# Macaron layer on Trainium2: the feed-forward halves unrolled, routed two batches at a time, expert weights applied by GpSimd

## The chip, the cores and the metric

The kernel runs on one core of a Trainium2 chip. The metric is the device time of the whole program in microseconds (us), from its first to its last instruction with what lies around them. Lower is better.

## What is computed

The input x has 8 batches of 512 tokens of 128 features, in float32. Three residual blocks follow each other: half a mixture-of-experts feed-forward, attention with 16 heads of 64, and the same feed-forward again. Only the feed-forward is touched by the change:

```python
x = x + 0.5 * ffn(layernorm(x)); x = x + attn(layernorm(x)); x = x + 0.5 * ffn(layernorm(x))
# ffn, over all N = 4096 tokens
scores = softmax(x @ gate_w.T); topk_w, topk_idx = top_k(scores, 2); topk_w /= topk_w.sum()
pos = cumsum(one_hot(topk_idx)) - 1; keep = pos < capacity       # capacity 1280 for each of 8 experts
comb = scatter(topk_w * keep)                                     # (N, 8)
y  = sum_e comb[:, e] * (silu(x @ we_gate[e].T) * (x @ we_up[e].T)) @ we_down[e].T
sh = silu(x @ ws_gate.T) * (x @ ws_up.T) @ ws_down.T              # shared, 256 wide = 2 groups
```

The running count in pos goes through all tokens in order, so batches have to be routed one after another.

## The kernel before

The work lies features by tokens: a batch is a 128x512 tile, one PSUM bank. The feed-forward has 10 groups per batch, 2 shared and 8 experts, each 128 wide. Every product that must hold float32 accuracy is made of three fp32r terms: both operands are split into a high part (a ScalarE copy to fp32r) and a low part (a subtraction), and high x high, low x high and high x low are added in one bank.

A group takes nine 512-column matmuls and this chain: gate product (L375), SiLU on ScalarE (L496), product with the up half on VectorE (`gated`, L635), for an expert the product with its weight row (`weighted`, L643), high part on ScalarE (L505), low part on GpSimd (L728), down product (L418). The weight row of an expert is spread over 128 partitions by a matmul of its own with a selection matrix (`weights`, L410). The down product of a group runs four groups behind its gate product (`LAG_Y`), the high part two groups behind.

Between the groups lie, for each batch: layer norm of a later batch on VectorE (L259, small steps L230 to L250, L265), transposes (L347), gate logits as three matmuls with 8 rows (L355), a ScalarE copy (L486) and transposes back (L362), some 20 small routing steps on VectorE (L562 to L616), among them four over all 8x8 pairs of experts (L576 to L582) that rank the scores, the positions by small matmuls (L382 to L387), transposes of three bf16 parts of the weights (L396), a copy (L622), the output's copy (L511), its transposes (L427) and the residual (L650).

Each engine runs a list written out by hand; semaphores connect them. `groups` runs the groups through a loop with a register for the batch; tables such as `ROUTE_AT` say at which group which small step stands. Attention is written out without loops and hands over when all of x is done (L650, last batch); the second feed-forward begins after attention's last residual (L1084).

Of the kernel before, what the change touches and what calls it, by code (L numbers as in the profile page):

```python
# [32 lines left out]
NH = 5  # L33
SETS = 3
SPLIT3 = 3
RSQRT_MAGIC = 0x5F3759DF
NEWTON = 3
ROUTE_STEPS = 21
LN_STAGES = 7 + 3 * NEWTON
LN_STEPS = TT + 7 + 2 + 4 * NEWTON + TT - 1  # L40
# [21 lines left out]
def macaron(nc, x, w_gate_up, w_down, gate_t, w_qk, w_v, w_out, b_out, fproj, bproj,  # L62
            rope, fourier, consts, consts_b, sel, rows, out):
    with ExitStack() as ctx:
# [3 lines left out]
        def sem(name):  # L68
# [9 lines left out]
        gate_hi = sb("gate_hi", [P, E], F32R)  # L78
        gate_lo = sb("gate_lo", [P, E], F32R)
# [9 lines left out]
        ident_b = sb("ident_b", [P, P], BF16)  # L89
        before_b = sb("before_b", [P, P], BF16)  # L90
        ones_b = sb("ones_b", [P, P], BF16)
        lower = sb("lower", [P, E, E])
        sel_b = sb("sel_b", [P, E, P], BF16)
# [5 lines left out]
                   sb(f"rs_{n}", [P, n]), sb(f"rsi_{n}", [P, n], I32), sb(f"nt_{n}", [P, 3, n])) for n in (TT, LATER)}  # L99
        stats, mean, rs = own[TT][0], own[TT][2], own[TT][4]  # L100
        stats_all, mean_all, rs_all = own[LATER][0], own[LATER][2], own[LATER][4]
# [6 lines left out]
        st_v = work[:, 4096:4096 + INNER]  # L108
        st_gu = work[:, 4096 + INNER:4096 + INNER + 2 * GROUPS * P]

        o_t = sb("o_t", [P, 2, T])
        comb_t = sb("comb_t", [P, T], BF16)
        route = sb("route", [P, 8, TT, E])
        rec_all = sb("rec_all", [P, 2, T])
        pairs = rec_all[:, 0].rearrange("p (n m) -> p n m", n=2)
        pair_gt, pair_ge = (pairs[:, n].rearrange("p (t a e) -> p t a e", t=TT, a=E) for n in range(2))
        small = sb("small", [P, 8, TT])
        mask_b = sb("mask_b", [P, TT, E], BF16)
# [3 lines left out]
        comb3 = sb("comb3", [P, TT, SPLIT3, E], BF16)  # L122
# [3 lines left out]
        hid_hi, hid_lo = qk_h[:, SETS - 1], qk_l[:, SETS - 1]  # L126
# [3 lines left out]
        act_g, prod = o_t[:, 0:2, :], turn[:, 1]  # L130
# [11 lines left out]
        st_down = work[:, 4096 + INNER + 2 * GROUPS * P:4096 + INNER + 3 * GROUPS * P]  # L142
        free = 4096 + INNER + 3 * GROUPS * P
        fourier_s, fproj_s = work[0:NF, free:free + T], work[0:NF, free + T:free + T + P]
# [6 lines left out]
        in_first, in_fourier, in_x0 = sem("in_first"), sem("in_fourier"), sem("in_x0")  # L151
# [9 lines left out]
        def setup_sync(sp):  # L161

            sp.dma_start(x_tok[:, 0], x[0].rearrange("(t p) d -> p t d", p=P)).then_inc(in_x0, 16)
            sp.dma_start(ident[:], consts[0]).then_inc(in_first, 16)
            sp.dma_start(gate_w[:], gate_t).then_inc(in_first, 16)
            sp.dma_start(st_gu, w_gate_up).then_inc(in_ffn, 16)
            sp.dma_start(fourier_s, fourier).then_inc(in_fourier, 16)
            sp.dma_start(fproj_s, fproj).then_inc(in_fourier, 16)
            sp.dma_start(bproj_s[:], bproj).then_inc(in_fourier, 16)
            sp.dma_start(lower[:].rearrange("p a b -> p (a b)"), consts[1][:, 0:E * E]).then_inc(in_small, 16)  # L170
            sp.dma_start(st_down, w_down).then_inc(in_ffn, 16)
            sp.dma_start(before_b[:], consts_b[0]).then_inc(in_small, 16)
            sp.dma_start(ident_b[:], consts_b[1]).then_inc(in_small, 16)
            sp.dma_start(sel_b[:].rearrange("p e m -> p (e m)"), sel).then_inc(in_small, 16)
            for b in range(1, B):
                sp.dma_start(x_tok[:, b], x[b].rearrange("(t p) d -> p t d", p=P)).then_inc(in_x, 16)
# [7 lines left out]
        def setup_act(act):  # L184
            act.wait_ge(in_first, 32)
            nc.scalar.activation(gate_hi[:], gate_w[:], ACT.Copy).then_inc(w_hi_ready, 1)

            act.wait_ge(in_fourier, 48)
            act.wait_ge(fenc_ps, 1)
            nc.scalar.activation(fenc[:], bank[6][:], ACT.Identity, bias=bproj_s[:, 0:1]).then_inc(fenc_ready, 1)  # L190
# [84 lines left out]


        def ffn(tag, last, follow=None):

# [1070 lines left out]
```

## Time and profile before

| | us |
|---|---|
| median of 3 runs (1409.71 to 1411.80) | 1411.39 |
| the profiled execution, its own time | 1412.86 |
| its span, first to last instruction | 1410.8 |
| first feed-forward, to its last residual | 260.8 |
| attention, from there to its last residual | 896.8 |
| second feed-forward, from there to its last residual | 249.7 |

The last three lines are differences of the starts of residual rows on VectorE (260.82, 1157.60, 1407.26). A profile page gives, for each engine, busy time, share of the span and instructions; a timeline row gives start, duration, engine, line, operation, output and inputs, and in brackets the idle time before it with what ended it. PE is TensorE, DVE is VectorE, ACT is ScalarE, POOL is GpSimd.

### The profile page before, as it was taken

Reading aid. Unit: us, or ns where it says so; the run is one execution under the profiler, and the core shown is the slowest. Engines: PE = TensorE matmul, PEld = TensorE weight load, DVE = VectorE, ACT = ScalarE, POOL = GpSimd, SP = SyncE. Lnnn points to the kernel's source line nnn. Section 1 sums busy time; section 2 is a strip of 40 time slices with the busy share of each in tenths; the row PEclk is TensorE's granted clock in tenths of the full one; section 3 lists DMA queues with packets and bytes.
Section 4 is the critical chain, followed back from the end, with each engine's and each line's share of the span. In section 5 each row is a group of like instructions: output and inputs, shape, how many; then the busy total and the mean of one; then the engine's idle time right before and its main releaser. Section 6 shows DMA issues by size and latency. Waiting matters only on the chain.

```text
span 1410.8 us, 25300 instructions
## 1 busy us (share of the span) xinstructions
PE 1297.9 (92%) x8258; PEld 828.9 (59%) x8258; DVE 1000.4 (71%) x1900; ACT 703.9 (50%) x1042; POOL 926.1 (66%) x684
## 2 busy tenths in 40 slices
PE   4999889689999999999999999999999937988997
PEld 2666666346656656666566566566566525666665
DVE  7889988687666666666666666666666426998896
ACT  3565555245455555555555545545545404555553
POOL 0444444577888888888888788788888512444444
PEclk9999999899999999999999999999999967999999
DMA  6000000123233232232232332332332210000000
GB/s 206 1 0 0 0 0 0 30 46 69 48 68 68 48 69 65 51 69 61 55 69 57 59 69 51 65 69 47 69 69 47 39 24 0 8 7 15 7 7 16
DMA packets 101418, 61.71 MB, mean 44 GB/s; under 512 B 75280, under 2 KB 84016, under 8 KB 101072
## 3 DMA queue, kind: packets, MB, share of 16 engines
q1 hardware_dynamic: 101328, 60.52, 19.8%
q8 instruction: 56, 0.92, 0.3%
q14 instruction: 34, 0.28, 0.1%
HBM read 24.30 MB, written 2.62 MB: 19 GB/s over the span
## 4 chain that ended last, share of the span: by engine, by line
PE 68%; DVE 8%; issue 3%; DMA 1%; DVEq 0%; POOL 0%; ACT 0%; SPq 0%; POOLq 0%; ACTq 0%
PE banks L919 16%; PE banks L902 13%; PE banks L934 6%; PE banks L878 6%; PE banks L843 6%; PE banks L907 4%; PE banks L375 4%; PE banks L943 4%; PE banks L862 3%; PE banks L418 2%; PE banks L885 1%; PE banks L410 1%; DVE xn L265 1%; DVE neg_max L1064 1%; DVE work L643 1%
## 5 line engine op out<-in xcount | busy, mean ns | idle before, releaser
L728 POOL TENSOR_TENSOR qk_l<-work,qk_h 128x512 fp32r<-128x512 f32 x160 | 206.3, 1293 | 301.2 <-ACT qk_h L505 299.8
L1064 DVE TENSOR_REDUCE neg_max<-banks 128x2 f32<-128x1024 f32 x256 | 313.4, 1224 | 102.5 <-PE banks L878 96.3
L1000 ACT ACTIVATE work<-banks 128x1024 f32<-128x1024 f32 x256 | 250.1, 1025 | 168.3 <-PE banks L907 168.3
L1148 POOL TENSOR_TENSOR turn<-turn,side_turned 128x512 f32<-128x512 f32 x128 | 160.7, 1276 | 129.1 <-DMA side_turned<-side 129.1
L919 PE MATMUL banks<-work 128*64 128x512 f32 x1024 | 233.8, 598 | 0.0
L1142 POOL TENSOR_TENSOR turn<-turn,fenc 128x512 f32<-128x512 f32 x128 | 162.4, 1291 | 12.6 <-DVE side L1057 8.9
L1153 POOL TENSOR_TENSOR qk_l<-turn,qk_h 128x512 fp32r<-128x512 f32 x128 | 162.1, 1289 | 0.9 <-ACT qk_h L1005 0.9
L1158 POOL TENSOR_TENSOR work<-work 128x1024 f32<-128x1024 f32 x64 | 153.1, 2392 | 6.2 <-PE banks L919 6.2
L919 PEld LDWEIGHTS banks<-work 128*64 128x64 f32 x1024 | 67.8, 136 | 132.8 <-issue 110.0
L505 ACT ACTIVATE qk_h<-work 128x512 fp32r<-128x512 f32 x160 | 100.6, 629 | 71.5 <-DVE work L643 62.1
L375 PE MATMUL banks<-x_hi,gu_hi 128*128 (+1 forms) x320 | 133.5, 417 | 2.6 <-DVE work L635 2.2
L375 PE MATMUL banks<-x_hi,gu_lo 128*128 (+1 forms) x320 | 128.9, 403 | 0.0
L375 PE MATMUL banks<-x_lo,gu_hi 128*128 (+1 forms) x320 | 127.6, 399 | 0.0
L878 PE MATMUL banks<-qk_h 64*128 64x512 f32 x512 | 116.7, 452 | 11.3 <-DVE neg_max L1064 8.3
L496 ACT ACTIVATE o_t<-banks 128x512 f32<-128x512 f32 x160 | 94.7, 592 | 63.8 <-PE banks L375 54.0
L1070 DVE TENSOR_TENSOR shift<-banks,own_rows 128x512 fp32r<-128x512 f32 x64 | 44.2, 691 | 111.0 <-PE banks L885 111.0
L643 DVE TENSOR_TENSOR work<-turn,banks 128x512 f32<-128x512 f32 x128 | 87.4, 684 | 35.2 <-PE banks L410 29.1
L1005 ACT ACTIVATE qk_h<-turn 128x512 fp32r<-128x512 f32 x128 | 80.5, 629 | 53.6 <-POOL turn L1148 53.5
L902 PE MATMUL banks<-qk_h 64*128 64x512 f32 x512 | 101.9, 395 | 1.4 <-DVE side L1057 1.4
L1057 DVE TENSOR_TENSOR turn<-banks,rope_t 128x1024 f32<-128x1024 f32 x63 | 77.1, 1224 | 36.6 <-PE banks L843 35.5
L902 PE MATMUL banks<-qk_h,qk_l 64*128 64x512 f32 x512 | 101.3, 392 | 0.0
L902 PE MATMUL banks<-qk_l,qk_h 64*128 64x512 f32 x512 | 101.3, 392 | 0.0
(149 smaller groups left out, 2517.6 us busy)
## 6 DMA issues: line engine op xcount, KB each, us to landing
side_turned<-side SPq DMA_DIRECT2D x256, 128.0 KB, 3.1
rec_all<-rec_d SPq DMA_DIRECT2D x128, 128.0 KB, 3.0
x_tok<-in_x SPq DMA_DIRECT2D x8, 256.0 KB, 5.8
out<-x_tok SPq DMA_DIRECT2D x8, 256.0 KB, 2.3
work<-in_w_gate_up SPq DMA_DIRECT2D x1, 1280.0 KB, 6.6
work<-in_w_qk SPq DMA_DIRECT2D x1, 1024.0 KB, 7.1
den_d<-den_rows SPq DMA_DIRECT2D x64, 4.0 KB
den_c<-den_d SPq DMA_DIRECT2D x64, 4.0 KB, 1.9
```

The costliest lines, as they stand in the source:

```text
L375: ins = nc.tensor.matmul(dst[:], w[:, j + k, :], of_batch(a, b), start=(n == 0), stop=(n == 2))
L643: nc.vector.tensor_tensor(hid[:, k % NH, :], prod[:, k % 2, :], C[k % 2][:], ALU.mult).then_inc(s["hidden"], 1)
L728: nc.gpsimd.tensor_tensor(hid_lo[:, k % 2, :], hid[:, k % NH, :], hid_hi[:, k % 2, :], ALU.subtract).then_inc(s["hid_lo_ready"], 1)
L878: ins = nc.tensor.matmul(M2[:, h, :], qk_h[OWN[h], g % SETS, Q, qt * P:(qt + 1) * P], qk_h[OWN[h], g % SETS, K, :], start=True, stop=True)
L902: nc.tensor.matmul(S[kt][:, h, :], k[OWN[h], g % SETS, K, keys], q[OWN[h], g % SETS, Q, :], start=(i == 0), stop=False)
L919: ins = nc.tensor.matmul(O[OWN[h], :], v_all[:, kt, n * DH:(n + 1) * DH], pt[:, g % 2, kt, h * T:(h + 1) * T], start=(kt == 0), stop=(kt = ...
L1000: nc.scalar.activation(pt[:, g % 2, kt, :], S[kt].rearrange("p h q -> p (h q)"), ACT.Exp, scale=QSCALE).then_inc(s["probs"], 1)
L1064: nc.vector.tensor_reduce(neg_max[:, g % 2, qt::DH], M2, AX.X, ALU.max, negate=True).then_inc(s["maxes"], 1)
L1142: nc.gpsimd.tensor_tensor(turn[:, g % 2, part], turn[:, g % 2, part], fenc[:], ALU.add).then_inc(s["with_fourier"], 1)
L1148: nc.gpsimd.tensor_tensor(turn[:, g % 2, part], turn[:, g % 2, part], side_turned[:, part], ALU.add).then_inc(done, 1)
L1153: return nc.gpsimd.tensor_tensor(qk_l[:, g % SETS, part], turn[:, g % 2, part], qk_h[:, g % SETS, part], ALU.subtract)
L1158: nc.gpsimd.tensor_tensor(pt[:, g % 2, 0, :], pt[:, g % 2, 0, :], pt[:, g % 2, 1, :], ALU.add).then_inc(s["first_sum"], 1)
```

## The change

Only `ffn`, the setup and the first steps of attention that overlap the first feed-forward are rewritten.

- The loop over batches is gone: `UNITS` lists all 80 (batch, group) pairs, and each engine runs `period(i)` for i in that list. Of the first two batches the four shared groups come first, then the experts of each.
- Layer norm, softmax, ranking and positions are done for two batches (8 token tiles) at once, at fixed places in a window of 20 periods. The top two are found by maximum, comparison with the maximum and a code that breaks ties, in place of the 8x8 pairs. There are 24 routing stages per window (before 20 per batch).
- The logits come from 16 matmuls per window with the tokens stationary and 16 moving columns; the three matmuls, the copy and the transposes back are gone.
- The weight rows go through DRAM: one transpose (L398) and one ScalarE copy, one DMA out, then for each batch two DMAs of 1 MB that spread the rows over all partitions (`share_in`). The eight selection matmuls, the bf16 split, its transposes and L622 are gone.
- An expert's SiLU output is multiplied by its weight row on GpSimd (`weighted`, L709), and VectorE multiplies that by the up half (`gated`, L643). The low part of the product is subtracted on VectorE (`hidden_low`, L647) instead of GpSimd.
- The normalised tokens are written by ScalarE (`tokens`, L485, four per batch).
- The down product of a group stands two groups behind its gate product (`LAG` 2), the high part one.

```diff
-                    for k in range(OPEN, GROUPS):
-                        step(b, k, True, True)
...
+NORM_AT = {0: range(0, 4), 1: range(4, 10), 2: range(10, 16)}
+ROUTE_AT = {8: range(0, 4), 9: range(4, 9), 10: range(9, 14), 11: range(14, 19), 12: range(19, 22), 13: range(22, 24)}
+FIRST_ROUTE_AT = {0: range(4, 14), 1: range(14, 22), 2: range(22, 24)}
...
                 def period(i):
+                    if i < N:
+                        gate_up(i)
...
+                    if c < CHUNKS and q == LOGITS_AT:
+                        logits(c)
+                    if c < CHUNKS and q == POSITIONS_AT:
+                        positions(c)
+                    if c < CHUNKS and q == SHARES_AT:
+                        turn_shares(c)
+                    if i == FIRST_POSITIONS_AT:
+                        positions(0)
+                    if i == FIRST_SHARES_AT:
+                        turn_shares(0)
+                    if 0 <= i - LAG < N:
+                        down(i - LAG)
...
+                def gated(i):
...
+                    source = act_g[:, i % 2, :] if g < NSH else act_w[experts(i) % 2]
+                    tt(hid[i % NH], source, U[i % 2][:], ALU.mult).then_inc(s["gated"], 1)
+
+                def hidden_low(i):
+                    dve.wait_ge(s["hid_hi_ready"], i + 1)
+                    tt(hid_lo[:, i % 2, :], hid[i % NH], hid_hi[:, i % 2, :], ALU.subtract)\
+                        .then_inc(s["hid_lo_ready"], 1)
...
+                    if i < N:
+                        gated(i)
+                    c, q = chunk(i)
+                    if 0 <= i - 1 < N:
+                        hidden_low(i - 1)
...
-                    nc.gpsimd.tensor_tensor(hid_lo[:, k % 2, :], hid[:, k % NH, :], hid_hi[:, k % 2, :],
-                                            ALU.subtract).then_inc(s["hid_lo_ready"], 1)
...
+                    nc.gpsimd.tensor_tensor(tiled(act_w[experts(i) % 2]), tiled(act_g[:, i % 2, :]),
+                                            share[b % 2][:, (g - NSH) // HALF_E, :, (g - NSH) % HALF_E, :],
+                                            ALU.mult).then_inc(s["weighted"], 1)
```

VectorE's order for two expert groups in mid-stream, before (turn is the unweighted product, work the weighted one):

```order
L635 TENSOR_TENSOR turn<-o_t,banks 128x512
L639 REGISTER_ALU
L642 REGISTER_ALU
L643 TENSOR_TENSOR work<-turn,banks 128x512
```

and in the change (rec_all and den_rows hold GpSimd's weighted SiLU, qk_l the low part):

```order
L643 TENSOR_TENSOR o_raw<-rec_all,banks 128x512
L647 TENSOR_TENSOR qk_l<-turn,qk_h 128x512
L643 TENSOR_TENSOR o_raw<-den_rows,banks 128x512
L647 TENSOR_TENSOR qk_l<-o_raw,qk_h 128x512
```

Both large VectorE steps of a group read PSUM before; now the second reads two SBUF tiles.

VectorE's order at the opening, between the first group's product and the mask of the first batch, before:

```order
L635 TENSOR_TENSOR work<-o_t,banks 128x512
L215 TENSOR_TENSOR down_lo<-work,down_hi 128x1280
L584 TENSOR_REDUCE route<-rec_all 128x32
L259 BN_STATS stats<-x_tok 128x6 x4
L586 TENSOR_SCALAR mask_b<-route 128x32
```

and the start of the same piece in the change, in which 34 rows lie between the first product and the mask (L611):

```order
L643 TENSOR_TENSOR turn<-o_t,banks 128x512
L248 TENSOR_TENSOR down_lo<-work,down_hi 128x1280
L566 BN_STATS stats<-x_tok 128x6 x8
L263 TENSOR_TENSOR mv<-stats 128x8
L264 TENSOR_TENSOR mv<-stats 128x8
L265 TENSOR_TENSOR ve<-stats 128x8
L267 TENSOR_SCALAR mean<-mv 128x8
L268 TENSOR_SCALAR rs<-ve 128x8
L269 TENSOR_TENSOR nt<-mv 128x8
L271 SCALAR_TENSOR_TENSOR ve<-nt,rs 128x8
L591 TENSOR_REDUCE small<-side_turned 128x8
```

The norm of the next two batches now stands ahead of the first mask.

TensorE's order there (the shapes are output partitions by columns):

```order
L408 MATMUL banks<-qk_l,gu_hi 128x512
L384 MATMUL banks<-count_b,ones_b 128x64
L387 MATMUL banks<-mask_b,ones_b 128x56
L387 MATMUL banks<-mask_b,ones_b 128x48
L387 MATMUL banks<-mask_b,ones_b 128x40
L387 MATMUL banks<-mask_b,ones_b 128x32
L387 MATMUL banks<-mask_b,ones_b 128x24
L387 MATMUL banks<-mask_b,ones_b 128x16
L387 MATMUL banks<-mask_b,ones_b 128x8
L390 MATMUL banks<-mask_b,before_b 128x64
L408 MATMUL banks<-qk_h,gu_hi 128x512
```

The positions, which wait for the mask, now stand behind the second group's gate and up products and ahead of the third's; before, they stood behind two and a half groups.

## Rows read from the trace of the kernel before

**Rows 1.** Busy time, share and instructions of each engine (page).

```profile
PE 1297.9 (92%) x8258; PEld 828.9 (59%) x8258; DVE 1000.4 (71%) x1900; ACT 703.9 (50%) x1042; POOL 926.1 (66%) x684
```

**Rows 2.** One batch in mid-stream, busy time of each engine (windows).

```profile
108.19:136.89 28.70, 26.05 (x124) 18.71 (x122) 25.88 (x76) 15.95 (x28) 12.91 (x11) 1.00 0.00 0
```

**Rows 3.** Where batches 0, 2 and 6 begin and each feed-forward ends (timeline).

```profile
18.74 0.77 PE L375 MATMUL banks<-x_hi,gu_hi 128*128 128x512 f32 x1 [0.25 <-issue]
...
79.53 0.40 PE L375 MATMUL banks<-x_hi,gu_hi 128*128 x1
...
79.77 0.40 PE L375 MATMUL banks<-x_hi,gu_lo 128*128 x1
...
194.27 0.40 PE L375 MATMUL banks<-x_hi,gu_hi 128*128 x1
...
260.82 0.69 DVE L650 TENSOR_TENSOR x_tok<-banks,x_tok 128x512 f32<-128x512 f32 x1 [5.04 <-PE banks L427]
...
1169.55 0.78 PE L375 MATMUL banks<-x_hi,gu_hi 128*128 128x512 f32 x1
...
1229.59 0.40 PE L375 MATMUL banks<-x_hi,gu_hi 128*128 x1
...
1344.32 0.40 PE L375 MATMUL banks<-x_hi,gu_hi 128*128 x1
...
1407.26 0.69 DVE L650 TENSOR_TENSOR x_tok<-banks,x_tok 128x512 f32<-128x512 f32 x1 [5.04 <-PE banks L427]
```

**Rows 4.** TensorE in one batch, its waits and its transposes (timeline).

```profile
114.59 0.19 PE L382 MATMUL banks<-mask_b,before_b 128*128 128x32 bf16 x1 [0.88 <-DVE mask_b L586]
...
119.21 0.39 PE L396 MATMUL banks<-ident_b,comb 128*24 128x128 bf16 x4 [0.73 <-DVE comb L616]
...
122.01 0.39 PE L410 MATMUL banks<-comb_t,sel_b 128*128 128x512 bf16 x1 [1.03 <-DVE comb_t L622]
...
123.68 0.60 PE L347 MATMUL banks<-ident,xn 128*128 128x128 f32 x4
...
124.04 0.48 PE L375 MATMUL banks<-x_hi,gu_hi 128*128 x1
```

**Rows 5.** VectorE beside GpSimd, and the same line alone (timeline).

```profile
108.75 1.28 POOL L728 TENSOR_TENSOR qk_l<-work,qk_h 128x512 fp32r<-128x512 f32 x1 [0.17 <-ACT qk_h L505]
...
108.78 1.53 DVE L577 TENSOR_TENSOR rec_all<-route 128x256 f32<-128x256 f32 x1
...
20.41 0.42 DVE L577 TENSOR_TENSOR rec_all<-route 128x256 f32<-128x256 f32 x1
```

**Rows 6.** One group's chain at the end of the second feed-forward (timeline).

```profile
1395.90 0.39 PE L375 MATMUL banks<-x_lo,gu_hi 128*128 128x512 f32 x1
...
1396.33 0.60 ACT L496 ACTIVATE o_t<-banks 128x512 f32<-128x512 f32 x1 [0.41 <-PE banks L375]
...
1400.95 1.28 DVE L643 TENSOR_TENSOR work<-turn,banks 128x512 f32<-128x512 f32 x2
...
1402.37 1.27 POOL L728 TENSOR_TENSOR qk_l<-work,qk_h 128x512 fp32r<-128x512 f32 x1 [0.74 <-ACT qk_h L505]
```

**Rows 7.** Norm and transposes at the start of the second feed-forward (timeline).

```profile
1158.53 0.87 DVE L259 BATCH_NORM_STATS2 stats<-x_tok 128x6 f32<-128x128 f32 x4
...
1160.32 0.17 DVE L241 TENSOR_SCALAR rsi<-ve 128x4 int32<-128x4 int32 x1
...
1160.52 0.17 DVE L243 TENSOR_SCALAR rs<-rsi 128x4 int32<-128x4 int32 x1
...
1164.00 1.08 PE L347 MATMUL banks<-ident,xn 128*128 128x128 f32 x4 [6.50 <-DVE xn L265]
```

**Rows 8.** A split on VectorE, tokens on ScalarE (timeline), a large DMA (page).

```profile
22.35 1.48 DVE L215 TENSOR_TENSOR down_lo<-work,down_hi 128x1280 fp32r<-128x1280 f32 x1
...
336.75 1.64 ACT L1012 ACTIVATE xn<-x_tok,shift_all,rs 128x128 f32<-128x128 f32 x4
...
work<-in_w_gate_up SPq DMA_DIRECT2D x1, 1280.0 KB, 6.6
```

More of the change, by code:

```diff
@@ new lines, in chunk, with experts, nth_expert, last_of @@
+            def chunk(i):
+                return i // WINDOW + 1, i % WINDOW
+            def experts(i):
+                return sum(1 for b, g in UNITS[0:i] if g >= NSH)
+            def nth_expert(n):
+                return [i for i in range(N) if UNITS[i][1] >= NSH][n] if n >= 0 else -1
+            def last_of(b):
+                return max(i for i in range(N) if UNITS[i][0] == b)
+            def first_of(b):
+                return min(i for i in range(N) if UNITS[i][0] == b)
+            def turned_at(i):
+                return next((b for b in range(B) if last_of(b) + LAG + 1 == i), None)
@@ L466, in pe @@
                 after_attention(pe)
                 pe.wait_ge(in_first, 32)
[L468 removed]
+                for b in range(CB):
+                    front(b)
                 pe.wait_ge(w_lo_ready, 1)
[L470 to L472 removed]
                 pe.wait_ge(consts_ready, 5)
[L474 to L478 removed]
+                logits(0)
@@ new lines, in pe, with fronts_before, turns_before @@
+                pe.wait_ge(in_small, 16 * 2)
+                if not last:
+                    fourier_terms(pe)
+                    pe.wait_ge(w_lo_ready, 2)
+                    pe.wait_ge(fenc_ready, 1)
+                for i in range(N + LAG + 2):
+                    period(i)
+            def fronts_before(b):
+                at = last_of(b) + LAG + 1
+                return CB + sum(1 for i in range(at) if batch_at(i, FRONT_AT) is not None)
+            def turns_before(b):
+                at = next((i for i in range(N) if batch_at(i, FRONT_AT) == b), -1)
+                return sum(1 for i in range(at + 1) if turned_at(i) is not None)
@@ L531, in end @@
[L531 to L548 removed]
+                    nc.scalar.activation(xh(b), XT[:], ACT.Copy).then_inc(s["x_hi_ready"], 1)
@@ L742, in sync @@
-            def sync(sp):
+                if not last:
+                    dve.wait_ge(in_x0, 16 * CB)
+                for n in range(LN_STAGES):
+                    norm(n, 0)
+                if not last:
+                    gate_low(dve)
+                for b in range(CB):
+                    x_low(b)
+                if not last:
+                    gate_up_low(dve, 0)
+                    dve.wait_ge(in_x, 16 * (B - CB))
+                dve.wait_ge(in_small, 16 * 2)
+                for n in range(4):
+                    route(n, 0)
```

819 lines of the change are left out of this document (389 added, 430 removed).

## The prediction

> **What bounds the kernel now.** The page comes first: TensorE is busy 92% of the span, VectorE 71% [rows 1]. That mixes attention, which the change leaves alone, with the two feed-forwards, so the table of windows comes next: one batch takes 28.70 us, in which TensorE shows 26.05 us and VectorE 25.88 [rows 2]. Both are nearly full. The timeline tells what ends last. TensorE's matmuls start 0.23 us apart (79.53 to 79.77, [rows 3]); a group has nine of them, 2.10 us, and with the weight matmul of an expert 2.33. In each batch TensorE stands still three times, 0.88, 0.73 and 1.03 us, each time for a routing result of VectorE: the mask, the bf16 weights, their copy [rows 4]. So the groups are bound by TensorE and the gaps by VectorE's routing. From batch 2 to batch 6, four batches take 194.27 - 79.53 = 114.7 us, two of them 57.4 (second half: 1344.32 - 1229.59, the same) [rows 3].
>
> A third thing is seen in VectorE's rows: L577 takes 0.42 us alone and 1.53 us where GpSimd started 0.03 us ahead of it; it ends 0.28 us after GpSimd does [rows 5]. VectorE steps that read two SBUF tiles wait for a running GpSimd step. The large steps (L635, L643) read PSUM and are not held. The Trainium skill ("SBUF — State Buffer", Who interferes with whom) states this as a lock: a VectorE instruction with two SBUF inputs and a GpSimd instruction that reads SBUF exclude each other, in both directions. These rows agree for one direction; the other is not seen here.
>
> **What is taken off TensorE.** Per batch: eight weight matmuls, 8 x 0.23 = 1.9 us; twelve small transposes become four fewer for logits and four fewer for weights, at 0.09 each (four in 124.04 - 123.68 = 0.36 [rows 4]), 0.7 us; three logit matmuls (0.7) against sixteen small ones per two batches. Those have no row of their kind; the bounds are nearly nothing (16 of 512 columns) and 0.23 (a full one). I take 0.09, the transposes' pitch, since both load a 128-wide stationary tile each time: 1.4 us per two batches. TensorE's work falls from about 25.5 to 22.9 us per batch, which for 16 batches would be 41 us. The question is what VectorE, ScalarE and GpSimd let it have.
>
> **An expert's group in the change.** VectorE now does `gated` and `hidden_low`, the latter with two SBUF inputs, and GpSimd's `weighted` for the next group lies between them. Two large VectorE steps take 1.28 us where one takes 0.69, so they start 0.60 apart; a GpSimd step of this size takes 1.28 [rows 5, 6]. If the two exclude each other, the loop is 0.60 (gated) + 0.60 (hidden_low) + 1.28 (weighted) + 0.04 (hand-off) = 2.52 us. The chain gives nearly the same: the SiLU starts 0.43 us after the third gate matmul starts [rows 6], that is 0.90 after the group's start; SiLU 0.60, hand-off 0.08, GpSimd 1.28, 0.04, gated 0.60, hidden_low of the group before 0.69, 0.05: its down product starts 4.24 us into the group after it and takes 0.70. Two periods in 4.94 are 2.47. So an expert costs 2.52 where it cost 2.33; a shared group stays 2.10. Window of 20: 16 x 2.52 + 4 x 2.10 = 48.7 us.
>
> **What else a window holds.** Small dependent VectorE steps start 0.20 us apart (1160.32 to 1160.52 [rows 7]); with 64 elements 0.26.
> - Mask (period 12): TensorE comes to `positions` 1.4 us into its period, VectorE is at five routing stages (1.3) behind the group before, done 5.5 us after that group's start: 4.4 us for the period, +1.9.
> - Weights (period 14): the step before them reads two SBUF tiles and waits for GpSimd: +1.5.
> - Logits, 1.4 us against 0.4 of slack: +1.0.
> - Tokens on ScalarE, 1.64 us for four [rows 8], twice, ahead of the next SiLU: 2 x 1.2.
> - Statistics of eight tiles (0.87 for four [rows 7]) in a shared period: +0.4.
>
> Sum 7.2: a window takes 55.9 against 57.4, and the two middle windows of each feed-forward give 2.8 us. The residual, the low part of x and the statistics cost nothing more since they lie in the 1.28 us in which VectorE waits for GpSimd; without that cover they would cost 0.6 each.
>
> **The opening.** First gate product: four more statistics (0.87), a second set of tokens (1.64), its transposes at the lower clock (1.08 for four against 0.60 [rows 4]) and its copy come before the logits, which save a copy and transposes: +3.0 in each half. Then TensorE runs two groups (2.8 us) and meets `positions`. VectorE reaches the mask after: first product at 3.0 (before, the down split follows it at 22.35 [rows 8], so it starts at 21.75, 3.0 after 18.74 [rows 3]), 0.6, the down split 1.4 (1.48 [rows 8]), statistics 1.6, three norm stages 0.8, ten routing stages 2.5, a product and a subtraction 1.2, the second half of the gate split 1.4, six norm stages 1.3, five routing stages 1.3: 15.1. The wait is 11.5 us allowing for the slower clock, 8.7 in the second half, which has no splits. The third group then waits for the weights behind six norm stages: +4.9. The weights go out to DRAM and 1 MB comes back (1.28 MB took 6.6 us [rows 8]), about 9 us with both hand-offs, of which three groups hide some 5: +4. First window: 48.7 + 7.2 + 11.5 + 4.9 + 4 = 76.3 against 79.53 - 18.74 = 60.8, +15.5; second half 73.5 against 1229.59 - 1169.55 = 60.0, +13.5 [rows 3].
>
> **The end.** No routing follows the last two batches, and they have no window extras: 48.7 plus 5.5 for the last chain. Against 1407.26 - 1344.32 = 62.9 that is -8.7; in the first half attention's first norm and projections lie there too, about 6.5 us: 60.7 against 260.82 - 194.27 = 66.6, -5.9 [rows 3].
>
> **Sum.** First half 3.0 + 15.5 - 2.8 - 5.9 = +9.8; second 3.0 + 13.5 - 2.8 - 8.7 = +5.0; attention 0. Together +14.8 on the profiled execution's 1412.9; the median of the runs lies 1.5 below it, so 1411.4 + 14.8 = **1426 us**.
>
> By the skill's rule in both directions the sum stays. Were there no exclusion at all, it would be the second rival below.
>
> **Rivals.**
> 1. *Every routing step with two SBUF inputs waits for a GpSimd step* and all of that reaches TensorE. One such wait adds 1.1 us to L577 [rows 5], and thirteen of the 24 stages are of that kind. If three or four more in each of the six windows that have routing reach the chain, that is 4 us each: 1426 + 24 = 1450. For: [rows 5]. Against: during a window's shared groups GpSimd is idle, and I have charged the two that TensorE waits for.
> 2. *Faster:* GpSimd's product and VectorE's subtraction run beside each other, or start in an order in which neither waits, so the routing stages slip in. The place is the middle window: at 2.47 us per expert with the extras halved it takes 47.9 + 3.6 = 51.5, 4.4 less; six windows, openings included, give 26.4 and the two ends 0.8 each, 28 in all: 1398. It decides at 2.5 us less per window than I have (14.8 / 6). For: TensorE has 2.6 us less work per batch. Against: [rows 5], and the chain alone holds 2.47.
> 3. *Balance:* windows near 53.4 us pay for the openings, 1411. That is how it would look if the small logit matmuls cost next to nothing and most of the tokens' time were hidden.
>
> **How the numbers follow.** Forecast (1414 to 1442) 0.58; rival 1 0.17; rival 2 0.18; rival 3 0.07. Within 0.2% (2.8 us, about what a measurement of this kernel can tell from no change) is 0.07, faster 0.18, slower 0.75. Unknown prices: logits at nothing or 0.23 per matmul, -11 or +18 us over eight rounds, less what waits cover, so -6 to +10; the return of the weights, 3 to 12 us each half. The range 1396 to 1452 takes in both rivals' values and leaves a fifth out.
>
> **What would show it.** Gate products of experts 2.5 us apart; `hidden_low` (L647) longer than 0.69 us or `weighted` late behind it; one TensorE wait of 9 to 12 us before L384 at each opening and one near 3 before L398; in mid-stream waits before L384 and L398 near 2; two batches near 56 us; the last two batches 6 to 9 us shorter than before. It would be wrong if experts ran 2.1 to 2.3 apart, if the opening wait were under 5 us, or if the logits L377 and L378 took over 3 us per window.

## The result, and the profile of the changed kernel

| | before | change | |
|---|---|---|---|
| median of 4 runs each (us) | 1410.55 | 1457.34 | ratio 1.0334, interval 1.0316 to 1.0352 |
| span of the profiled execution | 1410.8 | 1454.5 | +43.7 |
| first feed-forward, to its last residual | 260.8 | 283.6 | +22.8 |
| attention | 896.8 | 901.3 | +4.5 |
| second feed-forward | 249.7 | 266.2 | +16.5 |

The forecast was 1426 with a range of 1396 to 1452: the direction was right, the size was not. The page's first lines (busy time of each engine, and TensorE's granted clock in 40 slices) answer to [rows 1]:

```profile
PE 1298.6 (89%) x8082; PEld 843.5 (58%) x8082; DVE 914.3 (63%) x1504; ACT 698.6 (48%) x1076; POOL 890.5 (61%) x652
...
PEclk9799999969999999999999999999999956999999
...
work<-share SPq DMA_DIRECT2D x32, 1024.0 KB, 9.1
```

VectorE's busy time fell by 86 us, and the kernel became slower: less work on an engine gains nothing where the order of steps holds the time. The timeline rows that answer to [rows 3], the first gate products of each window of 20 groups (a "period" below is the time from one group's first gate product to the next's) and the residuals that end attention and both halves:

```profile
23.82 0.77 PE L408 MATMUL banks<-qk_h,gu_hi 128*128 128x512 f32 x1 [0.89 <-issue]
...
102.85 0.39 PE L408 MATMUL banks<-x_hi,gu_hi 128*128 128x512 f32 x1
...
221.02 0.40 PE L408 MATMUL banks<-x_hi,gu_hi 128*128 128x512 f32 x1
...
1202.18 0.77 PE L408 MATMUL banks<-qk_h,gu_hi 128*128 128x512 f32 x1
...
1278.89 0.39 PE L408 MATMUL banks<-x_hi,gu_hi 128*128 128x512 f32 x1
...
1337.68 0.40 PE L408 MATMUL banks<-qk_h,gu_hi 128*128 128x512 f32 x1
...
1396.43 0.39 PE L408 MATMUL banks<-x_hi,gu_hi 128*128 128x512 f32 x1
```

```profile
283.58 0.69 DVE L653 TENSOR_TENSOR x_tok<-banks,x_tok 128x512 f32<-128x512 f32 x1 [2.40 <-PE banks L428]
...
1184.88 0.69 DVE L1104 TENSOR_TENSOR x_tok<-banks,x_tok 128x512 f32<-128x512 f32 x1 [8.80 <-PE banks L963]
...
1451.05 0.69 DVE L653 TENSOR_TENSOR x_tok<-banks,x_tok 128x512 f32<-128x512 f32 x1 [2.40 <-PE banks L428]
```

From their differences, each against the same stretch of before:

| stretch | first half | forecast | second half | forecast |
|---|---|---|---|---|
| start | +5.1 | +3.0 | +5.3 | +3.0 |
| opening window | 79.0: +18.2 | +15.5 | 76.7: +16.7 | +13.5 |
| two middle windows | 118.2: +3.4 | -2.8 | 117.5: +2.8 | -2.8 |
| end | 62.6: -4.0 | -5.9 | 54.6: -8.3 | -8.7 |

With attention's +4.5 that makes the span's 43.7. The opening is where the time is; the middle is where the forecast had the wrong sign.

**The opening.** TensorE's first waits (timeline):

```profile
38.88 0.23 PE L384 MATMUL banks<-count_b,ones_b 128*128 128x64 bf16 x1 [10.51 <-DVE mask_b L611]
...
44.95 0.42 PE L398 MATMUL banks<-ident,comb_w 128*64 128x128 f32 x1 [2.84 <-DVE comb_w L625]
```

VectorE had its first product at 26.82 and the mask at 38.60, 11.8 us later, with the norm of the next batches in between. GpSimd's first product started at 54.52, 9.6 us behind the transpose of the weights at 44.95 (forecast: about 9). The 9.1 us of the page's line is the median of 32 transfers of 1 MB, of which up to four are issued together.

**Mid-stream.** Most experts are 2.47 to 2.6 us apart, as forecast. VectorE and GpSimd there (timeline):

```profile
1333.05 0.69 DVE L643 TENSOR_TENSOR turn<-den_rows,banks 128x512 f32<-128x512 f32 x1 [1.27 <-POOL den_rows L709]
1333.65 0.68 DVE L647 TENSOR_TENSOR qk_l<-turn,qk_h 128x512 fp32r<-128x512 f32 x1
1335.53 0.69 DVE L643 TENSOR_TENSOR o_raw<-rec_all,banks 128x512 f32<-128x512 f32 x1 [1.19 <-POOL rec_all L709]
```

```profile
1331.73 1.29 POOL L709 TENSOR_TENSOR den_rows<-o_t,work 128x512 f32<-128x512 f32 x1 [1.27 <-ACT o_t L508]
1334.21 1.29 POOL L709 TENSOR_TENSOR rec_all<-o_t,work 128x512 f32<-128x512 f32 x1 [1.19 <-ACT o_t L508]
```

VectorE stands still for 1.2 us in each group, waiting for the product, then does the product and the low part in one go; the low part of the group before had been free to start earlier but stands behind. These rows fit both explanations of the forecast, the chain (2.47) and the exclusion (2.52).

### The profile page after: what moved, and what is told of

It reads as the page before. It is cut to its first block and busy times, and to the rows that moved or that the text cites. A ratio compares the mean times of both kernels' runs of the same rounds, so it can differ in the third digit from the quotient of the medians.

```text
span 1454.5 us, 22616 instructions
## 1 busy us (share of the span) xinstructions
PE 1298.6 (89%) x8082; PEld 843.5 (58%) x8082; DVE 914.3 (63%) x1504; ACT 698.6 (48%) x1076; POOL 890.5 (61%) x652
## 5 line engine op out<-in xcount | busy, mean ns | idle before, releaser
L709 POOL TENSOR_TENSOR rec_all<-o_t,work 128x512 f32<-128x512 f32 x64 | 86.8, 1356 | 266.5 <-DMA work<-share 102.5
L1162 POOL TENSOR_TENSOR turn<-turn,fenc 128x512 f32<-128x512 f32 x128 | 162.1, 1291 | 16.5 <-DVE side L1077 11.1
L709 POOL TENSOR_TENSOR den_rows<-o_t,work 128x512 f32<-128x512 f32 x64 | 84.7, 1323 | 104.7 <-ACT o_t L508 104.7
L419 PE MATMUL banks<-qk_h,down_hi 128*128 128x512 f32 x160 | 78.2, 489 | 45.8 <-DVE qk_l L647 43.1
L927 PE MATMUL banks<-shift,ones_r 64*128 64x512 f32 x512 | 102.6, 393 | 0.0
L1185 POOL TENSOR_TENSOR o_t<-o_raw,rec_all 128x512 f32<-128x512 f32 x64 | 81.7, 1276 | 27.2 <-DMA rec_all<-rec_d 27.2
L954 PE MATMUL banks<-work,ones_f 128*32 128x256 f32 x1536 | 96.2, 383 | 0.1
```

What stands on the lines that cost most here:

```text
L709: nc.gpsimd.tensor_tensor(tiled(act_w[experts(i) % 2]), tiled(act_g[:, i % 2, :]), share[b % 2][:, (g - NSH) // HALF_E, :, (g - NSH) % HAL ...
L927: ins = nc.tensor.matmul(S[kt][:, h, :], ones_r[OWN[h], :], shift[OWN[h], g % 2, :], start=False, stop=True)
L954: ins = nc.tensor.matmul(W[c:c + 32, 0:HALF], ones_f[:], pt[:, g % 2, kt, first:first + HALF], start=(n == 0), stop=(n == 2))
L1162: nc.gpsimd.tensor_tensor(turn[:, g % 2, part], turn[:, g % 2, part], fenc[:], ALU.add).then_inc(s["with_fourier"], 1)
```

## The experiments

All are timed against the kernel before in the same session; ratios to be compared are those to before. Its median lay between 1410.55 and 1412.87 us in these sessions, so differences in us between two experiments carry some 2 us of that.

**1. The norm behind the first mask.**

```diff
-FIRST_ROUTE_AT = {0: range(4, 14), 1: range(14, 22), 2: range(22, 24)}
+FIRST_ROUTE_AT = {0: range(4, 19), 1: range(19, 24)}
+FIRST_NORM_AT = {1: range(0, 10), 2: range(10, 16)}
...
-                        for n in NORM_AT.get(q, ()):
+                        for n in (FIRST_NORM_AT if c == 1 else NORM_AT).get(q, ()):
```

> Change as it is, but in the opening of each half the norm of the next two batches stands behind the first mask and not ahead of it. Theory A (the opening's two long stalls are VectorE work that lies ahead of the mask): eight statistics and ten small norm stages, about 5 us, leave the path to the first positions; the second period falls from 12.7 and 10.4 us to about 8 and 6, the third stays near 7, and the whole time falls by 8 to 10 us, to 1448 (ratio to before near 1.027). Rival B (the norm only shifts the stall, since the tokens, the logits and the shares of the next batches come later by as much): the openings stay at 79 and 77 us and the time within 2 us of 1457.

1445.58 us, ratio 1.0226 (1.0208 to 1.0243). TensorE's waits in the first opening (timeline):

```profile
32.77 0.23 PE L385 MATMUL banks<-count_b,ones_b 128*128 128x64 bf16 x1 [3.41 <-DVE mask_b L612]
...
40.51 0.42 PE L399 MATMUL banks<-ident,comb_w 128*64 128x128 f32 x1 [4.50 <-DVE comb_w L626]
```

The wait for the mask fell from 10.51 to 3.41, the next one grew by 1.7; the opening windows measured 73.6 and 72.0, 5.4 and 4.7 less. The second period fell further than expected (to 6.5 and 5.5 us), but the third did not stay near 7: it grew from 7.3 and 6.6 to 8.9 and 7.6. Theory A holds: this much of the opening was order alone.

**2. The low part before the product.**

```diff
-                    if i < N:
-                        gated(i)
                     c, q = chunk(i)
                     if 0 <= i - 1 < N:
                         hidden_low(i - 1)
+                    if i < N:
+                        gated(i)
```

> Change as it is, but in a period VectorE subtracts the low part of the group before first and multiplies this group's product after it. Theory A (the chain of a group through the orders of the engines holds the 2.5 us of an expert): the low part no longer waits for the next group's GpSimd product, the down product two groups behind finds it ready, experts come 2.1 us apart, TensorE's own time; stages with fewer covers grow by part of it. A middle window falls from 59 to about 56, the end of the second half from 54.5 to about 49, the whole time by 20 to 30 us, to 1432 (ratio near 1.015). Rival B (GpSimd's product and VectorE's work exclude each other, 0.60 + 0.60 + 1.28 + 0.04 = 2.52, whatever their order): experts stay at 2.5 and the time at 1457.

1429.63 us, ratio 1.0112 (1.0091 to 1.0133): 28 us for the exchange of two steps, as theory A had it. The middle windows measured 56.3 to 57.9 and the second half's end 49.1. VectorE and GpSimd in the last window (timeline):

```profile
1410.73 0.88 DVE L647 TENSOR_TENSOR qk_l<-o_raw,qk_h 128x512 fp32r<-128x512 f32 x1 [0.70 <-ACT qk_h L513]
1411.54 0.68 DVE L643 TENSOR_TENSOR o_raw<-den_rows,banks 128x512 f32<-128x512 f32 x1
1412.91 0.85 DVE L647 TENSOR_TENSOR qk_l<-o_raw,qk_h 128x512 fp32r<-128x512 f32 x1 [0.70 <-ACT qk_h L513]
```

```profile
1409.77 1.30 POOL L709 TENSOR_TENSOR den_rows<-o_t,work 128x512 f32<-128x512 f32 x1 [0.88 <-ACT o_t L508]
1411.92 1.29 POOL L709 TENSOR_TENSOR rec_all<-o_t,work 128x512 f32<-128x512 f32 x1 [0.85 <-ACT o_t L508]
```

The low part now lies where GpSimd's product ends, takes 0.85 where it took 0.68, and the groups are 2.15 us apart. So at this place, where no routing stands, the exclusion costs a group some 0.2 us and does not hold it; the chain did, by the order of two VectorE steps (experiment 3 shows the same with that order left alone). Beside routing and norm steps the exclusion costs more: low parts there took up to 1.4 us. The 2.52 of the forecast was right as a number and half wrong as a reason: it took the exclusion for what holds the loop, and these groups come 2.15 apart with the exclusion in place.

**3. The down product three groups behind.**

```diff
-LAG = 2
+LAG = 3
-        hid_hi, hid_lo = qk_h[:, SETS - 1], qk_l[:, SETS - 1]
+        hid_hi, hid_lo = (q[:, 1:SETS].rearrange("p s q t -> p (s q) t") for q in (qk_h, qk_l))
```

(and the index i % 2 of these tiles becomes i % 3)

> Change as it is, but the down product stands three groups behind its gate product (LAG 3, three tiles for the high and low parts). Theory A (the chain): experts 2.1 us apart as TensorE allows; but VectorE then reaches the mask and the tokens' statistics with less time behind it, so the waits at the front (periods 3 and 4) and before positions (period 12) grow and the windows keep 57 to 59 us; the ends fall, the second half's from 54.5 to about 49. Whole time -10 to -14 us, 1445 (ratio near 1.024). Rival B (exclusion holds 2.52): experts stay at 2.5 and the time within 2 us of 1457. Rival C (TensorE time alone matters): windows of 48 and a time near 1400.

1436.79 us, ratio 1.0157 (1.0132 to 1.0182). Experts came 2.1 to 2.2 apart with VectorE's order unchanged, so it is the chain and not the exclusion that held them at 2.5. The middle windows measured 57.8 to 58.0: most of the slack went into new waits, as expected. The ends gave 3.8 and 5.7 us, the four middle windows 4.0 and the two openings 4.2, and the time fell by more than expected (20.6 us for 10 to 14). One of the new waits (timeline):

```profile
1342.53 0.87 PE L369 MATMUL banks<-ident,xn 128*128 128x128 f32 x3 [2.75 <-DVE x_tok L654]
```

One group more of lag brings the residual of the last batch into the period in front of the next transposes, which use the same bank.

**4. Positions and shares one period later.**

```diff
-LOGITS_AT, EXPS_AT, POSITIONS_AT, SHARES_AT = 8, 9, 12, 14
+LOGITS_AT, EXPS_AT, POSITIONS_AT, SHARES_AT = 8, 9, 13, 15
```

> Change as it is, but in mid-stream the positions stand in period 13 instead of 12 and the transpose of the weights in 15 instead of 14. Theory A (TensorE comes to both too early, by about 1.9 us each): the periods of 4.8 and 4.25 us fall by 2 in all per window, the six windows give 11 to 13 us: 1445 (ratio near 1.024). Rival B (the routing stages hold VectorE back by their own time wherever TensorE takes the result): the same extras appear one period later, within 3 us of 1457.

1446.20 us, ratio 1.0227 (1.0210 to 1.0245). Period 12 fell from 4.82 to 2.53, period 13 rose from 2.10 to 4.24, 14 fell from 4.25 to 2.68: middle windows 57.2 to 57.5 instead of 58.7 to 59.5. With the openings (76.9 and 73.5) that is 11.8 us, theory A's 11 to 13.

**5. Half of GpSimd's product.** On experiment 2, where experts come at nearly TensorE's pace; half of the experts' weights is left out:

```diff
-            share[b % 2][:, (g - NSH) // HALF_E, :, (g - NSH) % HALF_E, :],
+            share[b % 2][:, (g - NSH) // HALF_E, 0:TT // 2, (g - NSH) % HALF_E, :],
```

(the other operands are cut to the same half)

> e2_low_first, in which experts come 2.1 us apart, with GpSimd's product made over 256 of the 512 columns (the other half of each weighted tile is never written, so half of the experts' weights is left out). Theory A (VectorE's steps with two SBUF inputs wait for a running GpSimd product, and so the routing stages reach the mask, the weights and the tokens late): with products of 0.65 us the periods with extras shrink, 4.6 to 3.1, 6.0 to 4.6, 3.9 to 2.6; a middle window falls from 57.5 to about 51.6 and the time from 1430 by 28 to 36 us to 1397 (ratio near 0.989). Rival B (no such waiting matters; the extras are the stages' own length and TensorE's own small products): a middle window falls by less than 1 us, the time by less than 6.

1394.36 us, ratio 0.9872 (0.9837 to 0.9907). A middle window of the second half, of experiment 2 and of this one (windows: length, busy us and count of PE, PEld, DVE, ACT, POOL; clock; DMA share; GB/s):

```profile
1261.25:1317.59 56.34, 47.82 (x224) 36.62 (x222) 44.48 (x102) 31.82 (x57) 20.59 (x17) 1.00 0.29 83
```

```profile
1236.17:1288.35 52.18, 47.47 (x224) 37.09 (x222) 39.06 (x103) 30.90 (x56) 12.29 (x17) 1.00 0.27 90
```

VectorE's busy time fell by 5.4 us although it has the same steps: that is time in which it was held. The low parts (L647, here L648) account for 3.1 us of it (18.42 us in the first window, 15.36 in the second), smaller steps for the rest. One routing line over a whole run, of the change (in experiment 2 its longest is 710 ns) and of this kernel (the line's durations in ns: shortest, median, longest):

```profile
L602 DVE TENSOR_TENSOR side_turned<-side_turned,code x16: 213/225/1305, 32.6 to 1374.4; 128x64 f32<-128x64 f32 x16
```

```profile
L603 DVE TENSOR_TENSOR side_turned<-side_turned,code x16: 214/224/226, 32.7 to 1323.4; 128x64 f32<-128x64 f32 x16
```

All four middle windows are 52.2 where experiment 2 had 56.3 to 57.9. So GpSimd's full product costs a window 4 to 6 us in this order of steps. Part of that is the mechanism of the first rival, small VectorE steps that wait, and the larger part of the held time is the low parts. The halved product also shortens each group's chain by 0.55 us (1.29 to 0.74). At the second half's end, with the same groups and no routing, it gave 0.3 us (49.1 to 48.8), so there neither the shorter chain nor the shorter holds are worth much; for a window with routing these runs don't separate the two.

**6. Weight rows there from the start.** Both halves' first two batches read rows of x in place of the routed weights, which are left out there:

```diff
+                        if c == 0:
+                            of = x[b % CB, rows_of].rearrange("(t e) n -> t e n", t=TT).unsqueeze(0)
```

(and share_in of these batches no longer waits for share_out, which stands behind it)

> Change as it is, but the weight rows of the first two batches of each half are read from x instead of from the rows that the routing wrote (the transfers are as large, the values are not the weights; the routing itself stays), so that they are there before the first expert. Theory A: the first expert waits for the way out to DRAM and back; the sixth period of each half falls from 7.0 and 7.6 to about 2.6 us and the seventh by 1, so 4 to 5.5 us in each half, the time to 1448 (ratio near 1.027). Rival B (the down products, the tokens and the logits behind it have their own waits in these periods): under 2 us in each half.

1441.59 us, ratio 1.0203 (1.0165 to 1.0241). GpSimd's first products (timeline):

```profile
51.11 1.29 POOL L709 TENSOR_TENSOR rec_all<-o_t,work 128x512 f32<-128x512 f32 x1 [50.67 <-ACT o_t L508]
53.57 1.31 POOL L709 TENSOR_TENSOR den_rows<-o_t,work 128x512 f32<-128x512 f32 x1 [1.17 <-ACT o_t L508]
```

The openings fell from 79.0 and 76.7 to 72.0 and 72.5: the trip costs about 7.0 and 4.2 us, against a forecast of 4 each. The sixth period fell from 7.0 and 7.6 to 2.6 in both, as expected. Openings with no edit in them differ too: the first half's measured 77.7 in experiment 10's profile, so 1.3 of the 7.0 may be that. The rest of the 16 us is attention, 896.5 instead of 901.3, with no edit in it (experiment 10).

**7. Four moves together.** Experiments 1, 2 and 4, and the Fourier product behind the first group:

```diff
-                    fourier_terms(pe)
                     pe.wait_ge(w_lo_ready, 2)
-                    pe.wait_ge(fenc_ready, 1)
...
+                    if not last and i == 0:
+                        fourier_terms(pe)
```

> Three moves tested alone and one new one together: low part before the product, norm of the next batches behind the first mask (all first routing stages up to the mask in period 0), positions and shares one period later, and the Fourier product behind the first group. If their gains were independent: -28 (e2), -12 (e1), -11 (e4) and -1 to -3 for the Fourier product, 1457 - 53 = 1404. Theory A (with experts at 2.1 us a period hides less, but a stage that is late costs one wait only once): near that, 1393 to 1405, so 0.4 to 1.4% below before. Rival B (the waits share a cause, VectorE behind GpSimd, and move to the next place): 1415 to 1425, slower than before.

1402.23 us, ratio 0.9928 (0.9903 to 0.9952): faster than before. The gains nearly add (53 us expected of independence, 55 measured; by the ratios, 57 measured for 62 from experiments 1, 2 and 4). The first gate product moved from 23.82 to 20.95, and the first period grew from 2.70 to 4.84, so the Fourier product itself gained under 1 us.

**8. and 9. Other places in the window.** Experiment 8 is experiment 7 with the norm of the batches after next at the end of a window in place of the next ones' at its start, the second batch's tokens one period earlier, the weights' transpose in period 14, and the routing stages packed closer (`ROUTE_AT`, not shown):

```diff
-TOKENS_AT, FRONT_AT = (3, 5), (4, 6)
-LOGITS_AT, EXPS_AT, POSITIONS_AT, SHARES_AT = 8, 9, 13, 15
+TOKENS_AT, FRONT_AT = (3, 4), (4, 6)
+LOGITS_AT, EXPS_AT, POSITIONS_AT, SHARES_AT = 8, 9, 13, 14
+NEXT_NORM_AT = {16: range(0, 2), 17: range(2, 9), 18: range(9, 11), 19: range(11, 16)}
...
+                        for n in (NEXT_NORM_AT if c + 1 < CHUNKS else {}).get(q, ()):
+                            norm(n, c + 1)
```

> e7_four_moves with other places in the window: the norm of the batches after next at the end of a window instead of the next ones at its start, tokens of the second batch one period earlier, routing stages packed 6, 6, 5, transpose of the weights in period 14. Theory A: the front of a window (periods 3 to 5, 4.6 + 2.4 + 4.5 us in e2) loses about 4 of its 5 us of extras, since the tokens no longer wait for the norm; the statistics cost some 2.7 us at its end: windows from 53 to about 50, the time 12 to 16 us below e7's. Rival B (VectorE's stages cost the same wherever they stand): within 4 us of e7's.

1382.72 us, ratio 0.9791 (0.9759 to 0.9823). Experiment 9 spreads the norm over periods 13 to 19, puts shares back to 15, and moves some routing stages and five of the opening's norm stages (not shown):

```diff
-NEXT_NORM_AT = {16: range(0, 2), 17: range(2, 9), 18: range(9, 11), 19: range(11, 16)}
+NEXT_NORM_AT = {13: range(0, 1), 14: range(1, 4), 15: range(4, 7), 16: range(7, 9), 17: range(9, 12), 18: range(12, 14), 19: range(14, 16)}
```

> e8_tuned_places with the norm of the batches after next spread over periods 13 to 19 (the eight statistics in period 13, then one to three small stages each) and five of the opening's norm stages before its last routing stages. Theory A: the statistics no longer meet the last groups of a window (3.1 + 4.3 us in e8), windows fall from 52 to about 50.5 and the time by 5 to 9 us to 1376. Rival B (TensorE waits as long in period 13 as it did in 18 and 19): within 3 us of e8's 1383.

1371.86 us, ratio 0.9727 (0.9705 to 0.9750). The two moves gave 20 and 11 us for 12 to 16 and 5 to 9 expected. A middle window is 50.5 us:

```profile
1218.37:1268.87 50.50, 48.31 (x223) 36.74 (x222) 43.59 (x103) 31.86 (x57) 21.70 (x17) 1.00 0.24 89
```

TensorE shows 48.31 of 50.50. From the change to here 85 us came from the order of steps alone.

**10. Fills at attention's start.**

```diff
+                    for _ in range(n):
+                        nc.tensor.matmul(O, qk_hi[:, 0, 0, :], x2_hi[:, 0], start=True, stop=True)
```

(n is 9 ahead of the first maxima, 4 ahead of the next ones and of the first transposes of maxima)

> Change as it is, but in attention's first three periods TensorE fills its waits before the maxima with products into a bank that nobody reads (37 of 512 columns, 8.6 us at 0.233). Theory A (attention took 901.3 us against 896.8 in before only because TensorE's granted clock fell again at its start): the clock stays up, products of these periods lie 0.23 apart and not 0.43, attention takes 892 to 896 us and the whole time falls by 5 to 9 us to 1450. Rival B (something that the change does holds attention back, or the fills get in the way): 900 us or more, the time within 2 us of 1457 or above.

1452.26 us, ratio 1.0285 (1.0262 to 1.0307). Twenty microseconds at the same place, 23 us behind the last residual, of the change and of this kernel (windows as above):

```profile
306.80:326.80 20.00, 15.11 (x72) 9.84 (x74) 15.05 (x19) 7.81 (x10) 11.34 (x9) 0.76 0.18 37
```

```profile
306.00:326.00 20.00, 16.58 (x93) 9.48 (x91) 16.49 (x21) 8.76 (x11) 12.59 (x11) 0.95 0.17 35
```

The third transpose of the maxima came 43.5 us behind the last residual instead of 46.8 (42.6 in before), with the granted clock at 0.95 in place of 0.76. The whole time fell: the intervals of 1.0334 and 1.0285 lie apart. Attention as a whole took 899.0, not 892 to 896: theory A in its direction, at most half in its size. Without any edit there, attention took between 896.5 and 903.8 us in the kernels 1 to 9: 900.4 to 903.8 in the four that reached the third transpose after 45.2 us or more, 896.5 to 898.8 in the other five (42.6 to 43.3). So 899.0 is about what an early third transpose goes with; the 2.3 us alone would be within this spread. What sets the clock in this stretch from kernel to kernel is not shown.

**11. Fills ahead of the logits too,** on experiment 9: seven products of ones_r with xh(0) into bank 0.

> e9_spread_places with the fills of e10_attention_fill and seven products between the first transposes and the logits of each half, where TensorE waits for tokens and splits (3.7 us in all). Theory A: the sixteen logit products lie 0.107 and not 0.214 us apart (1.7 us less), the first group runs at 0.23 (1 to 1.5 less), so 2 to 3 us in each half, with the fills in attention 4 to 8: 10 to 14 us below e9, near 1364. Rival B (the fills do not raise the clock in time and hold up the transposes): within 3 us of e9, or slower.

1371.54 us, ratio 0.9710 (0.9676 to 0.9743): no gain, rival B. Two of the sixteen logit products behind the fills (timeline):

```profile
15.51 2.06 PE L466 MATMUL banks<-qk_h,ones_r 128*128 128x512 f32 x4
17.36 0.35 PE L379 MATMUL banks<-gate_hl,qk_h 128*128 128x16 f32 x1
17.57 0.36 PE L380 MATMUL banks<-gate_hl,qk_l 128*128 128x16 f32 x1
```

They stay 0.21 apart. The fills of experiment 10 are in this kernel too; attention took 898.1 us (897.6 in experiment 9), so neither place gained.

**12. The second half's first norm in attention's tail,** on experiment 9:

```diff
+            SECOND_NORM_AT = {N - 2: range(0, 1), N - 1: range(1, 8), N: range(8, LN_STAGES)}
...
+                    for n in SECOND_NORM_AT.get(p, ()):
+                        ffn2["first_norm"](dve, n)
```

(and ScalarE writes the first batch's tokens ahead of its wait for attention's end)

> e9_spread_places with the norm of the second half's first two batches made in the last periods of attention (whose residuals for these batches are long done, while VectorE shows waits of 3 to 9 us between its steps there), and their first tokens ahead of ScalarE's wait for attention's end. In e9_spread_places the second half's first gate product starts 17.3 us after attention's last residual, of which 5.2 us are this norm and 2.0 the tokens. Theory A (the chain from the last residual to the first product holds the start): 17.3 falls to about 10 and the time by 6 to 8 us, from 1371.9 to 1365 (ratio near 0.9677). Rival B (the small steps hold attention's last residuals back, or the tokens' place holds the exponentials back): no gain or slower.

1364.67 us, ratio 0.9670 (0.9643 to 0.9698). The second half's first gate product starts 10.2 us behind attention's last residual instead of 17.3, as expected, and this is the best version: 3.3% below before, with nothing of the computation left out.

## Why the prediction was right in direction and wrong in size

The excess of 28.9 us over the forecast (43.7 against 14.8) divides by its own terms. (From 114.7 to twice 55.9 is 2.9 us and not 2.8, which changes nothing.)

**Right.** An expert's group: 2.52, measured 2.47 to 2.6 (though see experiments 2 and 3 for the reason). The mask in the opening: forecast 11.5 and 8.7, waits 10.51 and 7.31; the norm ahead of it was named as its cause, and moving it gave 5 us per half. No routing at the end: -8.7, measured -8.3 in the second half (in the first -5.9, measured -4.0). Of a window's extras, three terms are as forecast. The first middle window of the second half, period by period (each is the difference of two first gate products):

| what | periods | measured | base | extra | forecast |
|---|---|---|---|---|---|
| mask | 12, 13 | 4.82 + 2.09 | 5.04 | 1.9 | 1.9 |
| weights | 14, 15 | 4.29 + 2.08 | 5.04 | 1.3 | 1.5 |
| logits | 8, 9 | 3.88 + 2.10 | 5.04 | 0.9 | 1.0 |
| tokens and transposes | 3, 4, 5 | 4.68 + 3.65 + 2.54 | 7.56 | 3.3 | 2.4 |
| shared groups, with the statistics | 0, 1, 10, 11 | 2.59 + 2.09 + 2.95 + 2.63 | 8.40 | 1.9 | 0.4 |
| the rest | 2, 6, 7, 16 to 19 | 18.40 | 17.64 | 0.8 | 0 |

**The step that failed: "Sum 7.2: a window takes 55.9".** The sum is 10.1, and a window takes 58.7 to 59.5. Three parts were priced too low:

- Shared groups, 1.5 us over their 0.4. They were priced at TensorE's own time, "a shared group stays 2.10", but one that follows an expert inherits that expert's late low part. TensorE's wait for it in period 10 (timeline):

```profile
1310.48 0.50 PE L419 MATMUL banks<-qk_h,down_hi 128*128 128x512 f32 x1 [0.60 <-DVE qk_l L647]
```

With the low part first (experiment 2), periods 0 and 10 fell from 2.59 and 2.95 to 2.14 and 2.18. Period 11 did not (2.63 to 3.32); there routing stages stand.

- Tokens and transposes, 0.9 us over 2.4. They were priced by ScalarE's 1.64 us alone. The first wait there is another one: in period 3 TensorE waits for a low part that stands behind the norm's steps on VectorE. One of these steps and the low part itself were held beside GpSimd's products (timeline of GpSimd, VectorE and TensorE):

```profile
1285.20 1.48 POOL L709 TENSOR_TENSOR rec_all<-o_t,work 128x512 f32<-128x512 f32 x1 [5.91 <-DVE turn L643]
...
1285.45 1.25 DVE L274 TENSOR_SCALAR rsi<-ve 128x8 int32<-128x8 int32 x1
...
1287.97 1.26 POOL L709 TENSOR_TENSOR den_rows<-o_t,work 128x512 f32<-128x512 f32 x1 [1.29 <-ACT o_t L508]
...
1288.39 1.39 DVE L647 TENSOR_TENSOR qk_l<-turn,qk_h 128x512 fp32r<-128x512 f32 x1
...
1289.84 0.58 PE L419 MATMUL banks<-qk_h,down_hi 128*128 128x512 f32 x1 [1.89 <-DVE qk_l L647]
```

L274 took 1.25 us (0.17 where GpSimd is idle) and the low part 1.39 (0.68): 1.8 us on the way to this wait. L274 has one input; the forecast expected only steps with two SBUF inputs to be held.

- The rest, 0.8 us over nothing.

The four middle windows together are 12.1 us over four times 55.9, and the two opening windows 5.9 over their forecasts: 18 of the 29. If the openings carry the same 10.1 of extras, which was not measured apart, then beside 48.7 for the groups 20.2 and 17.9 us of stalls are left against a forecast of 20.4 and 17.6. Within them the third group's period was 7.26 and 6.58, so 5.2 and 4.5 over 2.10 for the forecast's 4.9 (TensorE's wait in it was 2.84, "near 3" as forecast), and the trip through DRAM 7.0 and 4.2 instead of 4.

**The start: +3.0, measured +5.1 and +5.3.** The sixteen logit products were priced at 0.09 us, a pitch of the higher clock. In the opening, TensorE has waited, and they lie 0.214 apart: 3.4 us instead of 1.4. That is one of the forecast's own signs of being wrong, logits of over 3 us. In mid-stream they lie 0.11 apart (1303.78, 1303.89, 1304.00 in the timeline), 1.8 us, where the price nearly held. TensorE at the second half's start, in the change (timeline):

```profile
1198.77 0.35 PE L377 MATMUL banks<-gate_hl,qk_h 128*128 128x16 f32 x1 [1.50 <-DVE qk_l L632]
1198.98 0.36 PE L378 MATMUL banks<-gate_hl,qk_l 128*128 128x16 f32 x1
1199.19 0.36 PE L377 MATMUL banks<-gate_hl,qk_h 128*128 128x16 f32 x1
...
1202.18 0.77 PE L408 MATMUL banks<-qk_h,gu_hi 128*128 128x512 f32 x1
```

**Attention 0, measured +4.5.** In this execution products lie 0.43 us apart again from 38 us into attention, and 0.23 in before. That term was not in the sum, since attention is not edited; but its time is not fixed by its code (experiment 10). Why the clock fell there after this feed-forward stays open.

**The rivals.** The first (1450) was nearest. Its mechanism is real, and with 4 us per window it came close to the measured 3. In each middle window of the second half three small steps of the change were held (L274, L602, L624), 3.2 us together, and one low part, 0.7. Of these the forecast charged only L624, ahead of the weights. L274 lies ahead of the 1.89 us wait above, and L602 ahead of the mask (timeline):

```profile
1374.39 1.30 DVE L602 TENSOR_TENSOR side_turned<-side_turned,code 128x64 f32<-128x64 f32 x1
...
1376.24 0.23 DVE L611 TENSOR_TENSOR mask_b<-side_turned 128x64 bf16<-128x64 f32 x1
```

The mask's 1.9 us were thus right in size with 1.1 us of exclusion in them that the forecast did not name. How much of a window's excess the exclusion is, no run on the change's own order separates. The balance and the faster case assumed smaller extras; they were larger than priced. The exclusion "in both directions" that the forecast cites is seen too: GpSimd's product takes 1.56 us where VectorE's low part started 0.26 us ahead of it, and 1.29 otherwise (timeline of the change, VectorE and then GpSimd):

```profile
149.82 0.68 DVE L647 TENSOR_TENSOR qk_l<-turn,qk_h 128x512 fp32r<-128x512 f32 x1
```

```profile
147.89 1.29 POOL L709 TENSOR_TENSOR rec_all<-o_t,work 128x512 f32<-128x512 f32 x1 [2.22 <-ACT o_t L508]
150.08 1.56 POOL L709 TENSOR_TENSOR den_rows<-o_t,work 128x512 f32<-128x512 f32 x1 [0.90 <-ACT o_t L508]
```

That agrees with the Trainium skill ("SBUF — State Buffer", Who interferes with whom) in the direction that the trace of before did not show.

## What to carry to other kernels

When work is moved between engines, write down for each engine in what order a group's late step and the next group's early step stand: here two lines exchanged on VectorE were worth 28 us. Price extras also in periods that seem free, look for small VectorE steps that can start beside a long GpSimd step (0.2 us became 1.3 here), and price small products at the clock that their place has. Where a rewrite is slower, try its tables before its idea: with the same computation, places alone took this one from 3.3% slower to 3.3% faster.

## What was not expected of the hardware

- Behind the sixteen logit products of an opening, and in experiment 11 behind seven 512-column products and these sixteen, TensorE was still at the lower of its two clocks, 1.2 GHz: the first gate products lie 0.43 apart, where they lie 0.23 apart in mid-stream. In the second half's opening the granted clock is shown as 0.50 there; in the first half's it is shown as 1.00 at the same spacing, so the spacing of equal products is the better sign.
- Attention, with not a line of it edited, took 896.5 to 903.8 us over nine kernels, with its first 45 us at different clocks. A comparison of two kernels by one profile each can carry up to 7 us of that.
- The weight rows add 32 DMAs of 1 MB to the program. In experiment 9's middle window (89 GB/s) TensorE still shows 48.3 of 50.5 us, so next to them at most 2.2 us of it stood idle. No run shows the window without them.
